# Two-layer macaron kernel, Mamba stage: token normalisation and weighting of expert rows on ScalarE, their addition on VectorE in 512-wide instructions

## The chip, the cores and the metric

The kernel runs on one core of a Trainium2 chip. The metric is the device time of one execution in microseconds (us), taken as the median of several runs. The engines are TensorE (PE in the profile, PEld its weight loads), VectorE (DVE), ScalarE (ACT), GpSimd (POOL) and SyncE (SP), which only issues transfers here.

## The reference, cut to what matters

The input is 4 sequences of 1024 tokens with 128 features. Six blocks follow one another, each added to a running x:

```
x = x + 0.5 * moe(layernorm(x))        # 8 experts, 2 of them per token, and a shared one
x = x + mamba(layernorm(x))            # the stage that is changed: forward and reversed scan
x = x + 0.5 * moe(layernorm(x))
x = x + 0.5 * ternary(layernorm(x))
x = x + attention(layernorm(x))
x = x + 0.5 * ternary(layernorm(x))

layernorm(x) = (x - mean) / sqrt(var + 1e-5)
moe: out = shared(x) + sum over the two chosen experts of w[token, expert] * h[token, expert]
mamba, per direction:
  xs, z = split(h @ in_proj.T);  xs = silu(causal_conv(xs) + b)
  dt = softplus(x_proj(xs) ...);  state = exp(dt * A) * state + dt * xs * B;  y = sum_n state_n * C_n
  y = (y + xs * D) * silu(z);  out = y @ out_proj.T
```

## The kernel before

The tokens lie in SBUF as 32 tiles of 128 tokens (tokens on the partitions), and four tiles make a block of 512. The MoE stage writes each token's two expert outputs to HBM (`orows`), sorted by expert. They are added late: the weighted sum of the first MoE is done inside the Mamba stage, while that stage already runs.

`Returned` holds this return. `fetch` issues one gather on GpSimd for 128 rows into a ring of four buffers; a block takes eight gathers. `combine` (L105 to L118) runs on VectorE: it waits for the eight landings, and then does eight `scalar_tensor_tensor` of 128x128 (row times weight plus x), four for the first expert and, after a wait for these, four for the second. The last one and `s_read` free the ring buffer. The same `combine` is also used by the ternary stage for the second MoE.

The Mamba stage (`mamba`, L1090) makes 16 scan blocks b = 0 to 15: four per sequence (two directions, two halves of 512 tokens), each with 16 slots v, one per state index, and in each slot two halves of the 256 inner channels. A slot is, per half: ScalarE makes exp(dt*A) (`decay`, L1446), eight instructions ahead at most; TensorE broadcasts B into PSUM (`rows`, L1276, two slots ahead, in a ring of three); VectorE multiplies u by B (L1551) and scans (L1527); GpSimd multiplies the state by C (L1634); TensorE adds this to Y in PSUM (`add_y`, L1339). Every engine has its program written out in order, so that the order of the slots is the order of each queue.

Between these, the preparation of later blocks is put in slots by hand. `uses_of` says which use of the one PSUM bank O is in which slot: "T" the transposition of the normalised tokens, "x" the convolution, "z", "xp", "dt" the projections, "out" the output. Steps of the chain have a lag in slots on each engine. The softplus of a "dt" use is four instructions on ScalarE and four of 128x512 on GpSimd (L1660, L1656, L1651, and L1645, which makes u).

At the beginning of a block b, TensorE finishes Y of the block before, does a "dt" use (L1309), and then opens the next Y with matmuls of `diag` and, for the reversed direction, of the saved ys (`open_y`, L1329 and L1331). These can start only when Y has been read: in blocks with b % 4 of 1 and 2 ScalarE has copied Y out (L1453, in its slot 1, behind the "dt" reads and two decays), and in blocks with b % 4 of 3 and 0 VectorE has gated it (`gate`, L1507, behind the scans of its slot 1). The matmul for B of slot 4 (L1276) stands behind `open_y` in TensorE's queue.

The parts that the change touches, all before in VectorE's queue:
- `returned(n)`: 0 and 1 ahead of the scans, 2 to 7 in slots (0,4), (1,6), (2,6), (3,10), (4,10) and (5,10), given as (block, slot) in `RETURNS`.
- `statistics`: mean and variance of the tiles; then GpSimd's `root` (L1604 and L1606) makes 1/sqrt(var+eps), five times in all: twice ahead of the scans and in slots (1,10), (3,14) and (5,14).
- `normalize` (L1497): four `tensor_scalar` of 128x128, SBUF to SBUF. It is called eight times: for the first two blocks of tokens ahead of the scans, and then in slot 0 of scan blocks 2, 3, 6, 7, 10 and 11, for the transposition in slot 2.

Of the kernel before, what the change touches and what calls it, by code (L numbers as in the profile page):

```python
# [10 lines left out]
ALU = mybir.AluOpType  # L11
AX = mybir.AxisListType.X

P = 128
# [31 lines left out]
class Phase:  # L46
# [11 lines left out]
    def sem(self, name):  # L58
        s = self.ctx.enter_context(self.nc.semaphore(f"{self.tag}_{name}"))
        self.sems.append(s)  # L60
        return s
# [23 lines left out]
class Returned:  # L85
# [10 lines left out]
    def fetch(self, pool, ring, s_read, b, n):  # L96
        c, t = n // TPB, n % TPB
        if n == 0 and b >= 4:
            pool.wait_ge(s_read, b - 3)
        col = c * TILES + b * TPB + t  # L100
        pool.indirect_dma_start(ring[:, b % 4, n * P:(n + 1) * P], None, self.orows,
                                bass.IndirectOffsetOnAxis(ap=self.didx[:, col:col + 1], axis=0))\
            .then_inc(self.landed[b % 4], 16)

# [985 lines left out]
def mamba(nc, tag, x, ident, w, back):  # L1090
# [72 lines left out]
    with ExitStack() as ctx:  # L1163
# [45 lines left out]
        s_read = sem("read")  # L1209
# [40 lines left out]
        with nc.Block() as block:  # L1250
# [114 lines left out]
            def _(act):  # L1365
# [7 lines left out]
                act.activation(wzh[:], wi[:, 256:512], ACT.Copy).then_inc(s_wh, 1)  # L1373
                act.wait_ge(s_wc, 1)
# [80 lines left out]
                for b in range(-1, NB + 1):  # L1455
# [5 lines left out]
                    for v in range(NS):  # L1461
                        if v - 1 in uses:
                            o_read(b, v - 1, uses[v - 1])
# [12 lines left out]
            def _(dve):  # L1476
                ch = Chain(dve, s_gch)

                def returned(b):
                    back.combine(dve, ring, s_read, x, b, ch)  # L1480
# [10 lines left out]

                def normalize(tb):
                    i, _, c = place(tb)
                    dve.wait_ge(s_rstd, i + 2 if i else c + 1)
                    for t in range(TPB):
                        tile = i * TPS + c * TPB + t
                        last = dve.tensor_scalar(xn[:, t, :], x[:, tile * P:(tile + 1) * P], mv[:, tile, 0:1],  # L1497
                                                 rstd[:, tile:tile + 1], ALU.subtract, ALU.mult)
                    last.then_inc(s_xn, 1)
# [35 lines left out]
                normalize(0)  # L1535
# [4 lines left out]
                for b in range(-1, NB + 1):  # L1540
                    uses = uses_of(b)
                    for v in range(NS):
# [21 lines left out]
                        if b > 0 and slot_of(b, -2, "T")(v):  # L1564
                            normalize(uses[v + 2][2])
# [11 lines left out]
                        if (b, v) == (-1, 3):  # L1577
# [12 lines left out]
                            normalize(1)  # L1590

            @block.gpsimd
            def _(pool):
# [7 lines left out]
                def root(n):  # L1601
# [3 lines left out]
                    pool.wait_ge(s_ve, n + 1)  # L1605
                    pool.tensor_tensor(rstd[:, t], veps[:, t], mhalf[:, t], ALU.pow).then_inc(s_rstd, 1)  # L1606
# [808 lines left out]
```

## Time and profile before

| | |
|---|---|
| median of 3 runs | 3117.87 us (3114.83 to 3124.79) |
| span of the profiled execution, its one recorded time | 3183.4 us |
| busy in the span | PE 2649.1, DVE 2342.8, ACT 1746.4, POOL 1430.6 us |
| head of the Mamba stage, up to the first scan | about 335 to 400 us of the span |
| its 16 scan blocks | about 400 to 1420 us |
| mean granted TensorE clock | 0.913 |

The profile has one execution. Busy time is the time in which an engine has an instruction running; an instruction that waits inside the engine (for a port, say) counts as busy, one that waits for a semaphore counts as idle. For the idle time the profile names the releaser, the instruction whose end let the engine go on. The times of lines under one another in the timeline are from the start of the span; several instructions of one line that follow each other are one row (xN).

### The profile page before, as it was taken

How to read it: one execution, taken by the hardware profiler on the slowest of the kernel's cores; microseconds unless marked ns; L12 is line 12 of the kernel's file. 1: busy time of each engine (PE TensorE's matmuls, PEld its weight loads, DVE VectorE, ACT ScalarE, POOL GpSimd, SP SyncE). 2: the span in 40 equal slices, each digit the busy share in tenths (PEclk: the TensorE clock that was granted, in tenths of full speed). 3: DMA queues.
4: the chain of work that ended last, by engine and by line, in shares of the span. 5: the costliest groups of instructions: out<-in, count | busy, mean ns of one | idle time of the engine just before them, and what ended most of it. 6: DMA issues, size and time to landing. Idle time of an engine off the chain costs nothing. (4 is left out here: it accounts for less than half of the span.)

```text
span 3183.4 us, 38531 instructions
## 1 busy us (share of the span) xinstructions
PE 2649.1 (83%) x11128; PEld 1684.0 (53%) x11128; DVE 2342.8 (74%) x4109; ACT 1746.4 (55%) x3003; POOL 1430.6 (45%) x1514
## 2 busy tenths in 40 slices
PE   6888378889889989867888589949888889885999
PEld 5666233333334334225766467736555556553877
DVE  6688279989999999987688544477878777764444
ACT  3467365546556646523566345536776667763554
POOL 2465578888878878863464440031211111110000
PEclk9899688989899989996899789969999999996999
DMA  2146222222222222211146200000000000001000
GB/s 66 34 131 133 76 62 64 70 64 72 64 70 72 72 67 70 73 57 54 36 134 115 66 26 1 0 12 1 1 1 2 2 1 1 1 1 37 7 7 13
DMA packets 99373, 146.10 MB, mean 46 GB/s; under 512 B 12892, under 2 KB 50524, under 8 KB 98980
## 3 DMA queue, kind: packets, MB, share of 16 engines
q1 hardware_dynamic: 82052, 98.41, 10.5%
q0 software_dynamic: 16608, 44.78, 6.4%
q8 instruction: 91, 1.49, 0.2%
q14 instruction: 110, 0.90, 0.1%
q10 hardware_dynamic: 512, 0.53, 0.1%
HBM read 124.78 MB, written 18.87 MB: 45 GB/s over the span
## 5 line engine op out<-in xcount | busy, mean ns | idle before, releaser
L1634 POOL TENSOR_TENSOR a_hc<-a_H,a_cb 128x512 f32<-128x512 f32 x512 | 622.4, 1226 | 191.0 <-DVE a_H L1527 160.5
L1339 PE MATMUL a_Y<-a_hc,ident 128*128 128x512 f32 x1024 | 533.1, 640 | 36.8 <-POOL a_hc L1634 34.8
L2074 DVE TENSOR_REDUCE a_mx<-a_W 128x1 f32<-128x512 f32 (+3 forms) x768 | 397.2, 550 | 159.0 <-PE a_W L1878 104.7
L1980 ACT ACTIVATE a_pt<-a_W 128x512 f32<-128x512 f32 (+3 forms) x768 | 353.2, 492 | 227.8 <-PE a_W L1891 224.9
L1446 ACT ACTIVATE a_dA<-a_dt,a_aneg 128x512 f32<-128x512 f32 x512 | 339.7, 714 | 207.9 <-DVE a_H L1527 114.8
L1339 PEld LDWEIGHTS a_Y<-a_hc,ident 128*128 128x128 f32 x1024 | 182.7, 196 | 264.7 <-POOL a_hc L1634 134.8
L1891 PE MATMUL a_W<-a_Q,a_K 128*128 128x512 f32 (+3 forms) x768 | 303.2, 400 | 4.4 <-issue 2.3
L2222 POOL TENSOR_TENSOR a_spare<-a_zero 128x1 f32<-128x1 f32 x128 | 27.1, 212 | 582.7 <-ACT a_pt L1980 582.7
L1875 PE MATMUL a_W<-a_K,a_Q 128*128 128x512 f32 (+3 forms) x768 | 274.9, 365 | 10.8 <-DVE a_mx L2074 10.5
L411 ACT ACTIVATE m_raw<-m_U,m_wg 128x512 f32<-128x512 f32 x248 | 173.6, 701 | 127.7 <-PE m_U L306 122.9
L1009 DVE TENSOR_TENSOR t_hl<-t_raw,t_hh 128x512 fp32r<-128x512 f32 x128 | 88.1, 691 | 209.3 <-ACT t_hh L924 184.6
L1551 DVE TENSOR_TENSOR a_bx<-a_u,a_Bp 128x512 f32<-128x512 f32 x256 | 173.7, 678 | 77.6 <-POOL a_u L1645 41.6
L682 POOL DMA_INDIRECT m_xg<-m_xrows,m_gidx x184 | 194.5, 1057 | 70.4 <-issue 54.9
L1891 PEld LDWEIGHTS a_W<-a_Q,a_K 128*128 128x128 f32 x768 | 146.9, 193 | 143.5 <-issue 67.0
L576 DVE TENSOR_TENSOR m_hl<-m_raw,m_hh 128x512 fp32r<-128x512 f32 x248 | 172.3, 695 | 61.0 <-ACT m_hh L415 50.3
L814 PE MATMUL t_U<-t_hh,t_wh 128*128 128x512 f32 x512 | 204.0, 398 | 0.2 <-issue 0.2
L816 PE MATMUL t_U<-t_hl,t_wh 128*128 128x512 f32 x512 | 202.2, 395 | 0.7 <-issue 0.7
L815 PE MATMUL t_U<-t_hh,t_wl 128*128 128x512 f32 x512 | 202.1, 395 | 0.0
L1907 PE MATMUL a_PV<-a_pt,a_V 128*32 128x512 f32 (+3 forms) x1536 | 168.2, 510 | 40.7 <-POOL a_pt L2225 39.7
L1276 PEld LDWEIGHTS a_Bp<-a_bcs,a_sel 64*128 64x128 f32 x256 | 48.4, 190 | 285.2 <-DVE a_H L1527 176.1
L1276 PE MATMUL a_Bp<-a_bcs,a_sel 64*128 64x512 f32 x256 | 130.5, 511 | 79.7 <-DVE a_H L1527 79.4
L923 ACT ACTIVATE t_raw<-t_U,t_scal 128x512 f32<-128x512 f32 x128 | 88.2, 689 | 194.2 <-PE t_U L816 162.5
(311 smaller groups left out, 6432.0 us busy)
## 6 DMA issues: line engine op xcount, KB each, us to landing
a_cb<-a_crow SPq DMA_DIRECT2D x256, 256.0 KB, 3.2
m_orows<-m_yt SPq DMA_DIRECT2D x46, 256.0 KB
t_wst<-ternary_w SPq DMA_DIRECT2D x22, 256.0 KB, 2.9
m_xrows<-m_pool SPq DMA_DIRECT2D x16, 256.0 KB, 2.3
m_xg<-m_xrows,m_gidx POOLq DMA_INDIRECT x184
out<-x SPq DMA_DIRECT2D x8, 256.0 KB, 2.3
m_wg<-moe_ws SPq DMA_DIRECT2D x2, 516.0 KB, 4.4
a_hc<-mamba_conv_rows SPq DMA_DIRECT2D x1, 1024.0 KB
```

The lines of the kernel that those rows point to most:

```text
L682: pool.indirect_dma_start(xg[:, j % NXG, t * P:(t + 1) * P], None, xrows, bass.IndirectOffsetOnAxis(ap=gidx[:, n:n + 1], axis=0))\
L814: pe.matmul(out, wh[:, piece, c], rhs_h, start=start, stop=False)
L815: pe.matmul(out, wl[:, piece, c], rhs_h, start=False, stop=False)
L816: return pe.matmul(out, wh[:, piece, c], rhs_l, start=False, stop=stop)
L1276: pe.matmul(Bp[:, Q % BRING, :], sel[:, Q % NS, :], bcs[:, Q // NS % 4, :], start=True, stop=True)\
L1339: pe.matmul(Y[:, h, :], ident[:], hc[:, g % HCRING, :], start=False, stop=v == NS - 1).then_inc(s_y, 1)
L1446: act.activation(dA[:, G % ARING, :], dt[:, b % 2, h, :], ACT.Exp, scale=aneg[:, d, h, v:v + 1]).then_inc(s_dA, 1)
L1634: pool.tensor_tensor(hc[:, G % HCRING, :], H[:, s, span], cb[:, v % RING, :], ALU.mult).then_inc(s_hc, 1)
L1875: mm = pe.matmul(out, Q[:, g * GH + j, tile(t)], K[:, g, c * BLK:c * BLK + cols], start=True, stop=not diag)
L1891: pe.matmul(W[:, 3 + u % 3, 0:BLK - r * P], K[:, g, tile(kt)], Q[:, g * GH + j, c * BLK + r * P:(c + 1) * BLK], start=True, stop=True).the ...
L1980: act.activation(pt[:, u % PR, 0:BLK - r * P], W[:, 3 + u % 3, 0:BLK - r * P], ACT.Exp).then_inc(s_exp, 1)
L2074: dve.tensor_reduce(dst, W[:, s % 3, 0:min(BLK, (t + 1) * P - c * BLK)], AX, ALU.max)\
```

## The change

VectorE's `combine` is replaced in the Mamba stage by `weigh` on ScalarE and `add` on VectorE. `weigh` multiplies the fetched rows by the token's weight in the ring buffer itself, with four activations of 128x128 for each of the two experts; `add` adds the weighted rows to x with two `tensor_tensor` of 128x512, the second of which waits for the first. For return n in slot v of VectorE, ScalarE weighs the first expert's rows in slot v-2 and the second's in slot v-1. The ternary stage keeps `combine`.

`normalize` moves to ScalarE, as four `Identity` activations with a scale (rstd) and a bias. The bias is -mean*rstd, which GpSimd's `root` now also makes, with two further instructions, in the place of the variance. Its slots stay; in ScalarE's queue it stands at the beginning of the slot, ahead of that slot's reads of O and its decays. The first one stands ahead of the copy of the convolution weights (L1375), and the second in slot 6 of the block -1, ahead of the read of the "xp" use.

```diff
+    def weigh(self, act, ring, b, c, s_weighed):
+        if c == 0:
+            act.wait_ge(self.landed[b % 4], 32 * TPB * (self.run * NBLK // 4 + b // 4 + 1))
+        for t in range(TPB):
+            n = b * TPB + t
+            at = (c * TPB + t) * P
+            last = act.activation(ring[:, b % 4, at:at + P], ring[:, b % 4, at:at + P], ACT.Copy,
+                                  scale=self.wab[:, c, n:n + 1])
+        last.then_inc(s_weighed, 1)
+
+    def add(self, dve, ring, s_weighed, s_read, x, b, ch):
+        xb = x[:, b * BLK:(b + 1) * BLK]
+        for c in range(2):
+            dve.wait_ge(s_weighed, 2 * b + c + 1)
+            last = dve.tensor_tensor(xb, xb, ring[:, b % 4, c * BLK:(c + 1) * BLK], ALU.add)
+            if c == 0:
+                ch.step(last)
+                ch.join()
+        last.then_inc(s_read, 1)
+        dve.wait_ge(s_read, b + 1)
...
+                def normalize(tb):
+                    i, _, c = place(tb)
+                    act.wait_ge(s_rstd, i + 2 if i else c + 1)
+                    for t in range(TPB):
+                        tile = i * TPS + c * TPB + t
+                        last = act.activation(xn[:, t, :], x[:, tile * P:(tile + 1) * P], ACT.Identity,
+                                              bias=mv[:, tile, 1:2], scale=rstd[:, tile:tile + 1])
+                    last.then_inc(s_xn, 1)
+
+                back.weigh(act, ring, 0, 0, s_weighed)
+                back.weigh(act, ring, 0, 1, s_weighed)
+                normalize(0)
...
+                        for c in range(2):
+                            if (b, v + 2 - c) in RETURNS:
+                                back.weigh(act, ring, RETURNS[b, v + 2 - c][0], c, s_weighed)
+                        if b > 0 and slot_of(b, -2, "T")(v):
+                            normalize(uses[v + 2][2])
+                        if (b, v) == (-1, 3):
+                            back.weigh(act, ring, 1, 0, s_weighed)
+                            back.weigh(act, ring, 1, 1, s_weighed)
+                        if (b, v) == (-1, 6):
+                            normalize(1)
...
                 def returned(b):
-                    back.combine(dve, ring, s_read, x, b, ch)
+                    back.add(dve, ring, s_weighed, s_read, x, b, ch)
...
-                        last = dve.tensor_scalar(xn[:, t, :], x[:, tile * P:(tile + 1) * P], mv[:, tile, 0:1],
-                                                 rstd[:, tile:tile + 1], ALU.subtract, ALU.mult)
...
                     pool.tensor_scalar(veps[:, t], mv[:, t, 1], EPS, None, ALU.add).then_inc(s_ve, 1)
-                    pool.wait_ge(s_ve, n + 1)
-                    pool.tensor_tensor(rstd[:, t], veps[:, t], mhalf[:, t], ALU.pow).then_inc(s_rstd, 1)
+                    pool.wait_ge(s_ve, 3 * n + 1)
+                    pool.tensor_tensor(rstd[:, t], veps[:, t], mhalf[:, t], ALU.pow).then_inc(s_ve, 1)
+                    pool.wait_ge(s_ve, 3 * n + 2)
+                    pool.tensor_tensor(mv[:, t, 1], mv[:, t, 0], rstd[:, t], ALU.mult).then_inc(s_ve, 1)
+                    pool.wait_ge(s_ve, 3 * n + 3)
+                    pool.tensor_scalar(mv[:, t, 1], mv[:, t, 1], -1.0, None, ALU.mult).then_inc(s_rstd, 1)
```

## Rows read from the trace of the kernel before

**Rows 1.** Busy time by stage: window, length, PE, PEld, DVE, ACT, POOL, clock, DMA.
```profile
335.00:400.00 65.00, 19.58 (x43) 9.92 (x43) 17.85 (x59) 21.66 (x35) 46.81 (x47) 0.55 0.29 81
400.00:1420.00 1020.00, 882.61 (x2034) 368.77 (x2035) 959.77 (x1171) 555.77 (x854) 824.08 (x688) 0.92 0.23 68
```

**Rows 2.** What VectorE waited for, 330 to 1425 us: total us, times, longest.
```profile
DVE a_bx L1551 <- POOL a_u L1645: 41.6, 7, 24.0
DVE a_bx L1551 <- PE a_Bp L1276: 35.9, 22, 5.4
```

**Rows 3.** Groups by line and shape, 400 to 1420 us: count, busy us, mean ns.
```profile
L112 DVE SCALAR_TENSOR_TENSOR x<-a_ring,m_wab,x 128x128 f32<-128x128 f32 x48 | 24.8, 577 | 0.2
L1497 DVE TENSOR_SCALAR a_xn<-x,a_mv,a_rstd 128x128 f32<-128x128 f32 x24 | 19.0, 852 | 0.0
```

**Rows 4.** Timeline of three returns (start us, length us), and GpSimd beside the second.
```profile
349.24 2.31 DVE L112 SCALAR_TENSOR_TENSOR x<-a_ring,m_wab,x 128x128 f32<-128x128 f32 x8 [19.74 <-DMA a_ring<-m_orows,m_didx]
...
499.64 5.42 DVE L112 SCALAR_TENSOR_TENSOR x<-a_ring,m_wab,x 128x128 f32<-128x128 f32 x8
501.65 1.29 POOL L1634 TENSOR_TENSOR a_hc<-a_H,a_cb 128x512 f32<-128x512 f32 x1
509.26 1.27 POOL L1634 TENSOR_TENSOR a_hc<-a_H,a_cb 128x512 f32<-128x512 f32 x1 [6.33 <-DVE a_H L1527]
...
732.04 3.13 DVE L112 SCALAR_TENSOR_TENSOR x<-a_ring,m_wab,x 128x128 f32<-128x128 f32 x8
```

**Rows 5.** Timeline of the beginning of block 10, which normalises.
```profile
1061.30 2.51 DVE L1497 TENSOR_SCALAR a_xn<-x,a_mv,a_rstd 128x128 f32<-128x128 f32 x4
...
1067.94 1.61 PE L1329 MATMUL a_Y<-a_xs,a_diag 128*128 128x512 f32 x2 [1.86 <-ACT a_ys L1453]
...
1075.52 0.69 DVE L1551 TENSOR_TENSOR a_bx<-a_u,a_Bp 128x512 f32<-128x512 f32 x1 [1.45 <-PE a_Bp L1276]
```

**Rows 6.** The same of block 14, which does not normalise.
```profile
1304.23 0.67 DVE L1551 TENSOR_TENSOR a_bx<-a_u,a_Bp 128x512 f32<-128x512 f32 x1
...
1310.91 2.08 PE L1329 MATMUL a_Y<-a_xs,a_diag 128*128 128x512 f32 x2 [3.12 <-ACT a_ys L1453]
...
1318.41 0.69 DVE L1551 TENSOR_TENSOR a_bx<-a_u,a_Bp 128x512 f32<-128x512 f32 x1 [3.84 <-PE a_Bp L1276]
```

**Rows 7.** Blocks 11 (which normalises) and 15 (which does not).
```profile
1120.64 2.05 DVE L1497 TENSOR_SCALAR a_xn<-x,a_mv,a_rstd 128x128 f32<-128x128 f32 x4
1127.47 2.08 PE L1329 MATMUL a_Y<-a_xs,a_diag 128*128 128x512 f32 x2 [2.46 <-DVE a_ys L1507]
...
1362.91 0.68 DVE L1551 TENSOR_TENSOR a_bx<-a_u,a_Bp 128x512 f32<-128x512 f32 x1
1367.77 2.08 PE L1329 MATMUL a_Y<-a_xs,a_diag 128*128 128x512 f32 x2 [2.45 <-DVE a_ys L1507]
```

**Rows 8.** Blocks 2 and 3: the two longest normalisations, and block 2's opening of Y.
```profile
545.66 4.57 DVE L1497 TENSOR_SCALAR a_xn<-x,a_mv,a_rstd 128x128 f32<-128x128 f32 x4
554.35 2.08 PE L1329 MATMUL a_Y<-a_xs,a_diag 128*128 128x512 f32 x2 [1.85 <-ACT a_ys L1453]
614.52 3.88 DVE L1497 TENSOR_SCALAR a_xn<-x,a_mv,a_rstd 128x128 f32<-128x128 f32 x4
```

**Rows 9.** Groups by shape that stand nearest to the new instructions: busy us, mean ns.
```profile
L1980 ACT ACTIVATE a_pt<-a_W 128x128 f32<-128x128 f32 x128 | 33.4, 281 | 48.2 <-PE a_W L1891 47.6
L576 DVE TENSOR_TENSOR m_hl<-m_raw,m_hh 128x512 fp32r<-128x512 f32 x248 | 172.3, 695 | 61.0 <-ACT m_hh L415 50.3 <-issue 8.3
L1604 POOL TENSOR_SCALAR a_veps<-a_mv 128x8 f32<-128x8 f32 x3 | 0.8, 250 | 0.0
```

**Rows 10.** Timeline of the head: weight copy, first convolution, read of "xp".
```profile
355.56 1.91 ACT L1375 ACTIVATE a_wch<-a_hc 128x2048 fp32r<-128x2048 f32 x1 [14.07 <-DVE a_hc L1533]
360.88 0.76 PE L1294 MATMUL a_O<-a_xh,a_wch 128*128 128x512 f32 x1 [3.09 <-DVE a_xl L1570]
376.86 0.59 ACT L1394 ACTIVATE a_dbl<-a_O 72x512 f32<-72x512 f32 x1 [2.54 <-PE a_O L1305]
```

More of the change, by code:

```diff
@@ L1208, in mamba @@
         s_gch = sem("gch")
-        s_read = sem("read")
+        s_read, s_weighed = sem("read"), sem("weighed")
         s_pad, s_xn, s_xh = sem("pad"), sem("xn"), sem("xh")
@@ L1490, in statistics @@
                     last.then_inc(s_mv, 1)
[L1492 to L1496, printed above, removed]
-                        last = dve.tensor_scalar(xn[:, t, :], x[:, tile * P:(tile + 1) * P], mv[:, tile, 0:1],
-                                                 rstd[:, tile:tile + 1], ALU.subtract, ALU.mult)
-                    last.then_inc(s_xn, 1)
                 def gate(b):
@@ L1534, in _ @@
                 last.then_inc(s_wc, 1)
-                normalize(0)
                 dve.wait_ge(s_wh, 2)
@@ L1563, in _ @@
                             gate(b - 1)
-                        if b > 0 and slot_of(b, -2, "T")(v):
-                            normalize(uses[v + 2][2])
                         if slot_of(b, 2, "T")(v):
@@ L1589, in _ @@
                             dve.tensor_copy(sel[:], sels).then_inc(s_pre, 1)
-                            normalize(1)
             @block.gpsimd
```

## The prediction

> **What bounds the kernel now.** I read the busy time by stage first. In the head of the Mamba stage (335 to 400 us) no engine is full: a chain of dependent steps sets its length. In the 16 scan blocks (400 to 1420 us) VectorE is busy for 959.77 of 1020 us, GpSimd for 824.08 and ScalarE for 555.77 [rows 1]. VectorE is the bound there, and ScalarE has room. All that the change does lies in these 1085 us; the rest of the span stays as it is.
>
> Second come VectorE's waits. They show where it is not the bound: 41.6 us for GpSimd's u, of which 24.0 are the end of the head and the rest mostly ends of the early blocks, and 35.9 us in 22 waits for TensorE's broadcast of B [rows 2]. Looking for where these 22 stand, I found one around slot 4 of nearly every block. That decides most of what follows: VectorE time that is saved between the start of a block and slot 4 may only lengthen this wait.
>
> Third, the groups by line: 48 weighting instructions take 24.8 us and 24 normalising ones 19.0 us in the scan blocks [rows 3]. That is 577 and 852 ns each, more than they take alone: the eight of return 0, with no compute of GpSimd beside them, take 2.31 us [rows 4]. The timeline of return 3 shows why. It takes 5.42 us, and GpSimd is at work until 501.65+1.29 = 502.94; by the unmerged rows the first of the eight lasts until 503.09. So it sat in the engine until GpSimd had run its queue dry, about 3.1 us [rows 4]. Six returns are 13.9 us of work at 2.31 each, and 10.9 us of such waiting; the normalisations, at about 1.1 us of work each, are 6.6 us of work and 12.4 us of waiting.
>
> **The returns in the scan blocks (six).** Eight instructions become two of 128x512 with two SBUF inputs; such a one takes 0.695 us [rows 9]. With the wait of the second for the first, that is 1.45 us in place of 2.31: 0.86 saved. The wait for GpSimd remains, since the adds, like what they replace, read x and the ring in SBUF. In the three returns where GpSimd has a queue (499.64 and two more of 5 us) I take 0.9 saved. In the other three, as at 732.04 (3.13 us), it is now the first, short instruction that slips in ahead of GpSimd, and the second that waits; the same with the adds gives 0.69 + 1.1 + 0.69 = 2.5, so 0.6 saved. Sum: 3 x 0.9 + 3 x 0.6 = 4.5 us. Bounds: 24.8 - 6 x 1.45 = 16.1 us saved if the adds do not wait at all; 4.8 us lost if the second add of the three long returns has to wait 3.1 us again. All six stand behind slot 4's wait. GpSimd sits idle after them, 6.33 us after return 3 [rows 4], so that it follows VectorE at once, and I count the saving in full.
>
> The Trainium skill's page "SBUF — State Buffer", section "Who interferes with whom", says that `tensor_tensor` with both inputs in SBUF contends with GpSimd's reads, although it has no 2-port mode. By it the saving is that of the remaining waits, 4.5; without it, the 16.1. The trace has no such instruction against a queued GpSimd, only `scalar_tensor_tensor`, which waits. The same section says that the later one blocks until the first one finishes; here it was not one instruction but the whole queue, three of them [rows 4], and the measurement decides.
>
> **Normalisation in blocks 2, 6 and 10.** Here the trace has its own experiment. Blocks 10 and 14 have the same position in their sequence (b % 4 = 2), and block 14 has no normalisation. Counted from what follows the first scan (1061.30 and 1304.23), TensorE opens Y after 6.64 us in block 10 and after 6.68 in block 14, and VectorE gets its B of slot 4 after 14.22 and 14.18 us [rows 5, 6]. Block 10 spent 2.51 us normalising and waited 1.45; block 14 waited 3.84. The removed time comes back as waiting, to within 0.1 us: the chain is GpSimd's last products, TensorE's last adds, "dt", ScalarE's two reads, two decays and the copy of Y. In block 2 Y is opened 554.35 - 545.66 = 8.69 us after that point [rows 8], which is 2 us more than in block 10, because GpSimd is 2 us behind at its start and not because VectorE is. So of 4.57, 3.96 (block 6) and 2.51 us I count 0 as gained. Upper bound: all 11.0.
>
> **Normalisation in blocks 3, 7 and 11.** Here Y is freed by VectorE's own gate, behind the scans of slot 1. Block 11 opens Y 1127.47 - 1120.64 = 6.83 us after its first scan, block 15, without normalisation, 1367.77 - 1362.91 = 4.86 [rows 7]: 1.97 earlier, for 2.05 us of normalising. These are real gains: 2.0 in block 11, 2.0 in block 7 (2.04 there), and of block 3's 3.88 us [rows 8] about 3.8, since Y of block 2 is complete (617.5) before the gate would now come (about 618.1). Sum 7.8 us; lower bound 3.9, if GpSimd's backlog, which the stall lets it work off, takes half.
>
> **What ScalarE takes on.** A 128x128 activation takes 0.281 us [rows 9]. Eight per return and four per normalisation are 6 x 8 + 6 x 4 = 72, some 20 us over the scan blocks, on an engine that idles for 464 us there [rows 1]. What is queued behind them are the decays, which run mostly 6 to 18 us ahead of their scans, and the reads of O. Return 3's two packets stand in slots 4 and 5 of block 1, the others alike. Slot 0's normalisation comes before ScalarE's wait for "dt", in which it idles. The gathers landed long before. Cost 0; if that cover is gone, one packet of 1.1 us in each of six returns, 6.6 us.
>
> **GpSimd's `root`.** Two more instructions of about 0.25 us [rows 9], each behind a semaphore wait of 0.1: 0.65 us. In slots (1,10), (3,14) and (5,14) GpSimd is 2 to 7 us behind, and the end of blocks 1 and 3 and the opening of Y in block 6 wait for it: 3 x 0.65 = 1.9 us lost. Bounds 0 and 4 (if they meet VectorE's port use as well).
>
> **The head.** Weighing and adding return 0 takes, from landing, 4 x 0.28, and then the second four and an add: 2.9 us for 2.31, +0.6. `root` adds 0.65, so rstd comes at 355.7 instead of 354.4, and ScalarE normalises until 356.8. Only then can it copy the weights: 356.8 instead of 355.56 [rows 10]. The subtraction, xl and the first convolution at 360.88 follow: +1.3 us. Return 1 lands 1.2 us later by the same sum (about 368.7), and its eight activations end at 371.0, when the convolution that ScalarE reads next is also ready (371.1). The second normalisation, at about 376.4 to 377.5, ends before the read of "xp" (376.86 + 1.3 = 378.2). So +1.3, with bounds 0.3 and 5.
>
> **Sum.** -4.5 (returns) - 0 - 7.8 (normalisation) + 0 (ScalarE) + 1.9 (`root`) + 1.3 (head) = -9.1 us. In the profiled execution that is 3183.4 to 3174.3. The timed runs have their median at 3117.87, 2.1% under that span; I take the same microseconds there: 3109.
>
> **The rivals.** (1) More is gained: 0.20. Either blocks 2, 6 and 10 gain their 11.0 us too, or the adds don't wait for GpSimd's port (another 11.6); both come to about -20.5, 3097. For it: VectorE is 94% busy, and 44 us of its work are touched. Against it: rows 5 and 6, and what `scalar_tensor_tensor` did.
> (2) GpSimd takes over: 0.23. The stalls were the time in which it caught up, and its lag at the end of blocks 0 to 3 reaches 5 to 7 us. If the returns' and block 3's savings come back as waits for u (-8.3 not had), then -9.1 + 8.3 = -0.8, 3117. Against it: the 6.33 us of idle after return 3.
> (3) Slower: 0.07. The place is the join between the two adds. GpSimd's queue takes the port there, so that the second add of the three long returns waits 3.1 us again (+9.3), and with GpSimd the bound none of the 4.5 + 7.8 is realised: +1.9 + 1.3 + 9.3 = +12.5, 3130. It decides from the point where GpSimd has more queued at the join than it has idle time left in the block. Against it: between scans GpSimd gets new work only from VectorE, which stands still.
> The forecast itself has 0.50.
>
> **Numbers.** About 0.3% (9.4 us) is what this kernel's measurement can tell from no change. The forecast's own range is -4 to -14 and lies across that bound: half of its 0.50 is faster, half the same. Faster 0.25 + 0.20 = 0.45; same 0.25 + 0.23 = 0.48; slower 0.07. The range 3097 to 3121 holds (1) down to its point and (2), and leaves out (3).
>
> **What would show it.** The head: first scan 1 to 2 us later. Returns: two adds in 2.5 to 4.6 us. Blocks 10 and 14 of equal length but for VectorE's xl, with a wait of about 3.9 in both at slot 4; block 2's wait about 7. Blocks 7 and 11 shorter by 2, block 3 by 3 to 4. VectorE's busy time in the scan blocks down by some 23 us, while its wait for B rises by 11. The forecast is wrong if blocks 2, 6 and 10 get shorter by their stalls, if the adds take 1.45 us beside a busy GpSimd, or if the ends of blocks 0 to 3 wait longer for u by what was saved before.

## The result, and the profile after

The changed kernel takes 3106.22 us in the median of 6 runs (3100.84 to 3112.14), the kernel before 3118.59 in 6 runs on the same chip (3114.83 to 3126.70). The ratio is 0.9952, with a 95% interval of 0.9936 to 0.9967: 15 us faster, between 10 and 20 (the medians are 12.4 us apart). The forecast was 3109 (range 3097 to 3121).

The profiled execution of the changed kernel has a span of 3104.3 us, the one of the kernel before 3183.4. Most of these 79 us are not the change: experiment 8 shows a chip on which the kernel before takes this long, with the same stages longer, while its Mamba stage is as long as in the first profile to 1.3 us. The stage is therefore compared directly. From the first load of its weights to the first scan (the head) it takes 66.4 us for 64.8 before, and the 16 scan blocks take 1004.7 for 1019.2. Head and blocks together are 12.9 us shorter.

Busy time by stage (columns as in [rows 1], which it answers):

```profile
312.40:378.70 66.30, 17.90 (x43) 9.24 (x43) 14.33 (x39) 29.76 (x59) 47.43 (x51) 0.58 0.28 80
378.70:1383.50 1004.80, 877.43 (x2033) 366.07 (x2033) 934.85 (x1111) 576.84 (x926) 825.93 (x693) 0.93 0.24 69
```

VectorE has 24.9 us less to do in the scan blocks, ScalarE 21.1 more, and the blocks are 14.4 us shorter. VectorE's waits, 310 to 1390 us, as [rows 2]:

```profile
DVE a_bx L1585 <- PE a_Bp L1297: 43.2, 24, 6.2
DVE a_bx L1585 <- POOL a_u L1680: 41.3, 7, 24.6
DVE x L119 <- ACT a_ring L111: 30.6, 5, 20.9
```

The wait for B has grown from 35.9 to 43.2 us, the one for GpSimd's u has not grown in sum. The third line is nearly all the head. The groups of the moved work in the scan blocks, as [rows 3] and [rows 9]:

```profile
L119 DVE TENSOR_TENSOR x<-x,a_ring 128x512 f32<-128x512 f32 x12 | 19.0, 1586 | 0.6 <-ACT a_ring L111 0.4
L111 ACT ACTIVATE a_ring<-a_ring,m_wab 128x128 f32<-128x128 f32 x48 | 15.2, 389 | 0.0
L1401 ACT ACTIVATE a_xn<-x,a_mv,a_rstd 128x128 f32<-128x128 f32 x24 | 9.8, 478 | 0.0
L1641 POOL TENSOR_SCALAR a_mv<-a_mv 128x8 f32<-128x8 f32 x3 | 0.8, 261 | 0.3
L1639 POOL TENSOR_TENSOR a_mv<-a_mv,a_rstd 128x8 f32<-128x8 f32 x3 | 0.6, 205 | 0.2
```

An add takes 1.59 us in the mean for its 0.70 of work: it still waits for GpSimd. The timeline of return 3 (start, length), as [rows 4], shows it:

```profile
477.50 4.58 DVE L119 TENSOR_TENSOR x<-x,a_ring 128x512 f32<-128x512 f32 x2
479.52 1.28 POOL L1669 TENSOR_TENSOR a_hc<-a_H,a_cb 128x512 f32<-128x512 f32 x1
486.28 1.27 POOL L1669 TENSOR_TENSOR a_hc<-a_H,a_cb 128x512 f32<-128x512 f32 x1 [5.48 <-DVE a_H L1562]
```

GpSimd's queue ends at 480.80, and the first add at 481.36 by the unmerged rows, 0.56 us later, having started at 477.50; the second takes 0.70. The six returns now take 2.17, 4.58, 4.22, 4.17, 2.16 and 2.35 us, where they took 3.12, 5.42, 5.06, 4.97, 3.13 and 3.3: 5.3 us less.

Blocks 10 and 14, what opens Y and what ends the wait at slot 4, as [rows 5, 6]:

```profile
1035.99 2.07 PE L1350 MATMUL a_Y<-a_xs,a_diag 128*128 128x512 f32 x2 [3.12 <-ACT a_ys L1487]
1043.50 0.70 DVE L1585 TENSOR_TENSOR a_bx<-a_u,a_Bp 128x512 f32<-128x512 f32 x1 [3.83 <-PE a_Bp L1297]
...
1274.53 1.81 PE L1350 MATMUL a_Y<-a_xs,a_diag 128*128 128x512 f32 x2 [3.12 <-ACT a_ys L1487]
1282.11 0.70 DVE L1585 TENSOR_TENSOR a_bx<-a_u,a_Bp 128x512 f32<-128x512 f32 x1 [3.89 <-PE a_Bp L1297]
```

Block 10 now waits 3.83 us where it waited 1.45 and normalised for 2.51. Its length is 59.24 us for 59.28 before. Blocks 2 and 3, as [rows 8]; the last line is the end of block 3:

```profile
532.11 2.07 PE L1350 MATMUL a_Y<-a_xs,a_diag 128*128 128x512 f32 x2 [3.12 <-ACT a_ys L1487]
540.68 0.70 DVE L1585 TENSOR_TENSOR a_bx<-a_u,a_Bp 128x512 f32<-128x512 f32 x1 [6.19 <-PE a_Bp L1297]
...
596.28 1.12 PE L1350 MATMUL a_Y<-a_xs,a_diag 128*128 128x512 f32 x2
...
659.45 0.70 DVE L1585 TENSOR_TENSOR a_bx<-a_u,a_Bp 128x512 f32<-128x512 f32 x1 [6.04 <-POOL a_u L1680]
```

Block 11, as [rows 7]. Its first scan starts at 1087.45, and Y is opened 6.03 us later (8.02 before). Counted as in [rows 7], from what follows that scan (1088.63), it is 4.85 us for 6.83; block 15, which never normalised, had 4.86:

```profile
1092.17 1.26 DVE L1542 TENSOR_TENSOR a_ys<-a_zs,a_Y 128x512 f32<-128x512 f32 x2
1093.48 1.66 PE L1350 MATMUL a_Y<-a_xs,a_diag 128*128 128x512 f32 x2 [2.21 <-DVE a_ys L1542]
1101.06 0.70 DVE L1585 TENSOR_TENSOR a_bx<-a_u,a_Bp 128x512 f32<-128x512 f32 x1 [0.53 <-PE a_Bp L1297]
```

The head, as [rows 10]:

```profile
325.86 2.45 ACT L111 ACTIVATE a_ring<-a_ring,m_wab 128x128 f32<-128x128 f32 x8 [7.35 <-DMA a_ring<-m_orows,m_didx]
332.88 1.65 ACT L1401 ACTIVATE a_xn<-x,a_mv,a_rstd 128x128 f32<-128x128 f32 x4 [4.57 <-POOL a_mv L1641]
334.43 1.89 ACT L1409 ACTIVATE a_wch<-a_hc 128x2048 fp32r<-128x2048 f32 x1
339.73 0.76 PE L1315 MATMUL a_O<-a_xh,a_wch 128*128 128x512 f32 x1 [3.98 <-DVE a_xl L1602]
```

In block 0 there is a wait in slot 11 that the kernel before does not have:

```profile
423.20 0.69 DVE L1585 TENSOR_TENSOR a_bx<-a_u,a_Bp 128x512 f32<-128x512 f32 x1 [1.05 <-PE a_Bp L1297]
```

The length of each scan block, before, after and the difference in us:

```
block   0     1     2     3     4     5     6     7     8     9    10    11    12    13    14    15
before 74.76 69.34 68.80 76.82 65.04 62.71 62.19 63.42 57.99 58.65 59.28 64.93 60.08 58.65 58.62 57.88
after  74.51 69.04 67.97 71.58 60.68 62.48 62.73 61.73 60.11 58.65 59.24 61.73 58.91 58.65 58.69 58.03
diff   -0.25 -0.31 -0.83 -5.24 -4.36 -0.23 +0.54 -1.69 +2.12  0.00 -0.04 -3.20 -1.16  0.00 +0.07 +0.15
```

### The profile page after: what moved, and what is told of

The parts are those of the page before. It is cut to its first block and busy times, and to the rows that moved or that the text cites. A ratio compares the mean times of both kernels' runs of the same rounds, so it can differ in the third digit from the quotient of the medians.

```text
span 3104.3 us, 38566 instructions
## 1 busy us (share of the span) xinstructions
PE 2625.7 (85%) x11128; PEld 1673.7 (54%) x11128; DVE 2317.0 (75%) x4029; ACT 1777.0 (57%) x3099; POOL 1427.4 (46%) x1524
## 5 line engine op out<-in xcount | busy, mean ns | idle before, releaser
L1585 DVE TENSOR_TENSOR a_bx<-a_u,a_Bp 128x512 f32<-128x512 f32 x256 | 173.6, 678 | 84.6 <-PE a_Bp L1297 43.2
```

## The experiments

Each starts from the changed kernel. "Blocks" is the length of the 16 scan blocks in the trace of its run: before 1019.2, after 1004.7.

**1. Normalisation alone.** The returns go back to VectorE as one weighting instruction per row tile.

```diff
-                    back.add(dve, ring, s_weighed, s_read, x, b, ch)
+                    back.combine(dve, ring, s_read, x, b, ch)
```

(and ScalarE's five calls of `weigh` are gone.)

> Normalisation on ScalarE and the two further GpSimd instructions, but the returns as in the kernel before (eight weighted adds on VectorE). Theory (saved VectorE time counts only where VectorE stands in the chain): blocks 3, 7 and 11 shorter by 4, 2 and 2 us than before, blocks 2, 6 and 10 as before, +0.9 in the head, +1.9 for GpSimd: -5 us against before, about 0.9984 of it. Rival (VectorE is the bound and all its time counts): -19.0 + 2.8 = -16 us, 0.995.

Measured: 0.9989 (0.9976 to 1.0003) of before; blocks 1011.4, 7.8 shorter. Block 3 is 4.41 shorter, block 7 1.66, block 11 3.19; blocks 2, 6 and 10 change by -0.44, +0.60 and -0.03. The three blocks named gain 9.3 us together; blocks 4, 5, 8 and 12, where at most `root` is changed, differ by -2.2, +2.3, +2.1 and -1.2 (taken up below). The rival's 0.995 lies outside the interval. The time alone cannot be told from that of the kernel before.

**2. Returns alone.** The call moves from ScalarE's loop to VectorE's, and the old `normalize` and `root` are back.

```diff
-                        if b > 0 and slot_of(b, -2, "T")(v):
+                        if b > 0 and not (True) and slot_of(b, -2, "T")(v):
...
+                        if b > 0 and (True) and slot_of(b, -2, "T")(v):
+                            normalize(uses[v + 2][2])
```

> Returns weighed by ScalarE and added in two instructions, normalisation and GpSimd's root as in the kernel before. Theory: 4.5 us less in blocks 0 to 5, +0.6 in the head: -4 us against before, 0.9987. Rival (GpSimd takes the saved time back as waits for u at the ends of blocks 0, 1 and 3): 0 to -1 us. Rival (the adds have no port to wait for): -16 us, excluded already by the trace of after if its adds last 4 us there.

Measured: 0.9992 (0.9979 to 1.0005); blocks 1015.5, 3.7 shorter. The groups in its scan blocks:

```profile
L119 DVE TENSOR_TENSOR x<-x,a_ring 128x512 f32<-128x512 f32 x12 | 19.0, 1585 | 0.6 <-ACT a_ring L111 0.4
L1538 DVE TENSOR_SCALAR a_xn<-x,a_mv,a_rstd 128x128 f32<-128x128 f32 x24 | 19.1, 853 | 0.0
```

The adds cost the same 19.0 us with VectorE's normalisations beside them as without. The blocks with returns, 0 to 5, change by +0.04, -0.84, -2.09, -1.04, -3.14 and -0.96, and blocks 6, 7 and 8, which have none, are longer by 1.57, 1.56 and 2.14. Two of the six savings come back. In block 0 VectorE waits 1.04 us for B in slot 11, a wait that neither the kernel before nor experiment 1 has. After block 5, which is 0.96 shorter, block 6 opens Y 11.67 us after its first scan for 10.70: counted from block 5's first scan it is the same moment, 73.41 us for 73.40. The interval of the timed runs holds no change as well as the forecast of 0.9987.

**3. Only blocks 2, 6 and 10 normalise on VectorE again.**

```diff
-                        if b > 0 and slot_of(b, -2, "T")(v):
+                        if b > 0 and not (b % 4 == 2) and slot_of(b, -2, "T")(v):
...
+                        if b > 0 and (b % 4 == 2) and slot_of(b, -2, "T")(v):
+                            normalize(uses[v + 2][2])
```

> The changed kernel, but the normalisations of blocks 2, 6 and 10 done by VectorE again. Theory: the same time as the changed kernel; VectorE's wait at slot 4 of these blocks goes back from 6.8, 7.9 and 3.8 us to about 2.5, 2.9 and 1.4, and the blocks keep their lengths within 0.5 us. Rival (VectorE is the bound): these blocks are 3.6 us longer each and the whole 11 us longer than the changed kernel.

Measured: 0.9969 (0.9956 to 0.9982); blocks 1006.9. Against the changed kernel, blocks 2, 6 and 10 are -0.49, +0.22 and +0.06 us: the normalising of three blocks, put back, cost nothing. Their waits at slot 4 are 1.96, 3.66 and 1.45 us for 6.84, 7.23 and 3.83. The 2.2 us of the sum are block 4 (+2.47), which has no edit. Block 10, after its first scan:

```profile
1036.60 2.54 DVE L1541 TENSOR_SCALAR a_xn<-x,a_mv,a_rstd 128x128 f32<-128x128 f32 x4
...
1050.86 0.69 DVE L1594 TENSOR_TENSOR a_bx<-a_u,a_Bp 128x512 f32<-128x512 f32 x1 [1.45 <-PE a_Bp L1297]
```

The wait is 1.45 us again, to the hundredth that of [rows 5].

**4. Only blocks 3, 7 and 11 normalise on VectorE again.** The same edit with `b % 4 == 3`.

> The changed kernel, but the normalisations of blocks 3, 7 and 11 done by VectorE again. Theory: blocks 3, 7 and 11 are longer than in the changed kernel by 4, 2 and 2 us, as their gate comes later by that: +8 us in all. Rival (no normalisation in slot 0 is worth anything, the gain of blocks 3 and 11 came from TensorE's clock): the same time as the changed kernel.

Measured: 0.9986 (0.9975 to 0.9997); blocks 1013.9, 9.2 longer than the changed kernel's. Block 3 +5.39, block 7 +3.29, block 11 +3.04: 11.7 us. Block 8 is 3.65 shorter, so that blocks 7 and 8 together gain nothing from the normalisation's move: 121.5 us here, 121.8 in the changed kernel, 121.4 before. Block 11:

```profile
1100.10 2.05 DVE L1541 TENSOR_SCALAR a_xn<-x,a_mv,a_rstd 128x128 f32<-128x128 f32 x4
1106.93 2.07 PE L1350 MATMUL a_Y<-a_xs,a_diag 128*128 128x512 f32 x2 [2.46 <-DVE a_ys L1551]
1115.56 0.70 DVE L1594 TENSOR_TENSOR a_bx<-a_u,a_Bp 128x512 f32<-128x512 f32 x1 [1.58 <-PE a_Bp L1297]
```

With the 2.05 us of normalising, 1.05 us more of waiting at slot 4 come back (1.58 for 0.53). That is the part which the forecast did not have.

**5. The adds read PSUM.** In returns 2 to 7 the second operand is a PSUM tile; this kernel leaves out the adding of those returns' expert rows, and its time is to be read so.

```diff
-            last = dve.tensor_tensor(xb, xb, ring[:, b % 4, c * BLK:(c + 1) * BLK], ALU.add)
+            other = bx[:, 1, :] if bx is not None else ring[:, b % 4, c * BLK:(c + 1) * BLK]
+            last = dve.tensor_tensor(xb, xb, other, ALU.add)
...
-                    back.add(dve, ring, s_weighed, s_read, x, b, ch)
+                    back.add(dve, ring, s_weighed, s_read, x, b, ch, bx if b > 1 else None)
```

> The changed kernel, but the adds of returns 2 to 7 read their second operand from PSUM (a product tile) instead of the ring, so that each has one SBUF input; the expert rows of these six returns are fetched and weighed but not added, which this kernel leaves out. Theory (the adds' time above 1.45 us per return is the wait for GpSimd's port, as both operands are in SBUF): the six returns take 1.3 to 1.5 us each instead of 19.0 in all, GpSimd keeps its backlog and idles less behind them; the saved 10 us count, since GpSimd still runs dry in the block: 8 to 10 us under the changed kernel. Rival (GpSimd takes the time back at the ends of blocks 1 to 3): the adds get as short, but the waits for u grow and the total falls by 3 us or less. Rival (no port: the adds are long for another reason): they stay at 4.2 to 4.6 us in returns 3 to 5.

Measured: 0.9913 (0.9889 to 0.9938); blocks 992.8, 11.9 shorter than the changed kernel's. Return 3 and the group:

```profile
502.51 1.38 DVE L120 TENSOR_TENSOR x<-x,a_bx 128x512 f32<-128x512 f32 x2
503.32 1.27 POOL L1687 TENSOR_TENSOR a_dt<-a_rl,a_um 128x512 f32<-128x512 f32 x1
508.09 1.27 POOL L1670 TENSOR_TENSOR a_hc<-a_H,a_cb 128x512 f32<-128x512 f32 x1 [2.26 <-DVE a_H L1563]
...
L120 DVE TENSOR_TENSOR x<-x,a_bx 128x512 f32<-128x512 f32 x12 | 8.1, 674 | 0.6 <-ACT a_ring L111 0.5
```

Beside a GpSimd at work the two adds take 1.38 us, not 4.58. Of VectorE's time 10.9 us are gone, and all of it shows in the length (10.5 us against the changed kernel's second trace, experiment 9). So the adds' wait is the one for the port between GpSimd and two SBUF inputs, as the Trainium skill's page "SBUF — State Buffer", section "Who interferes with whom", says of `tensor_tensor`. GpSimd did not take over either: the adds of blocks 1, 2 and 3 take 3.2, 2.8 and 2.8 us less, and the blocks are shorter by 4.4, 3.6 and 2.8 against the first trace of the changed kernel and by 3.2, 2.7 and 2.8 against experiment 9's. GpSimd's idle time after return 3 fell from 5.48 to 2.26.

**6. GpSimd's `root` away from the slots where it is late.**

```diff
-        ROOTS = {(1, 10): 2, (3, 14): 3, (5, 14): 4}
+        ROOTS = {(1, 10): 2, (4, 3): 3, (6, 3): 4}
```

> The changed kernel with GpSimd's roots of slots (3,14) and (5,14) in slots (4,3) and (6,3), where nothing waits for them at once. Theory (they lie in GpSimd's backlog ahead of the block's end): block 3 shorter by 2.6 us, its wait for u down from 6.0 to about 3.5; block 6's opening of Y, at +11.2 us, earlier by up to 2.6; 3 to 5 us in all. Rival (GpSimd's root is hidden): no block changes by more than 0.5 us.

Measured, in one run with its trace (3165.65 us, for 3188.77 of the kernel before on the same chip): blocks 999.3, 5.4 shorter. Block 3 is 68.86 us for 71.58, block 6 60.49 for 62.73, the two blocks whose end or opening waited for it; but block 4, behind block 3, is 2.25 us longer, so that blocks 3 and 4 together gain only 0.5. The end of block 3, for the 6.04 us above:

```profile
679.34 0.69 DVE L1585 TENSOR_TENSOR a_bx<-a_u,a_Bp 128x512 f32<-128x512 f32 x1 [3.31 <-POOL a_u L1680]
```

**7. GpSimd issues the gathers in slots 1 to 8 of every block.** They stood in the odd slots up to 15.

```diff
-                        if v >= 7 if b < 0 else v % 2:
+                        if v >= 7 if b < 0 else 1 <= v <= 8:
```

> The changed kernel with GpSimd's gathers in slots 1 to 8 of each block instead of every second slot up to 15: four of them, 1.2 us each, leave the second half, where GpSimd falls behind. Theory (the waits for u and B at the ends of blocks 0, 1 and 3, 11.5, 3.5 and 6.0 us, are GpSimd's backlog): they shrink by up to 4.9 us each, 8 to 14 us in all, little of it lost in the first half, where GpSimd has slack. Rival (GpSimd's sum of work in the block decides, wherever it stands): the waits move to the middle of the blocks and the scans last as long, within 2 us.

Measured, in one run with its trace (3184.00 us, for 3188.77; outside the Mamba stage, the first ternary and the attention stage are 324.4 and 828.3 us, for 316.7 and 820.7 in experiment 6): blocks 996.9, 7.8 shorter, just under the 8 to 14 expected, and 6.4 shorter than experiment 9's. The end waits fell from 11.46 to 7.89 in block 0 (both with a wait in slot 11), from 3.50 to 1.08 in block 1 and from 1.25 to 0 in block 2. Block 3, against the expectation, is 1.3 us longer. Its end and a scan within it:

```profile
645.38 1.28 DVE L1562 TENSOR_TENSOR_SCAN a_H<-a_dA,a_H,a_bx 128x512 f32<-128x512 f32 x1 [1.13 <-POOL a_hc L1669]
...
680.39 0.70 DVE L1585 TENSOR_TENSOR a_bx<-a_u,a_Bp 128x512 f32<-128x512 f32 x1 [4.75 <-POOL a_u L1680]
```

With eight issues close together in the first half, one scan waits for GpSimd's product (1.13 us), VectorE waits 0.53 at slot 4 where it did not, and the adds of return 5 take 4.78 us for 4.17; the end wait fell only by 1.29. What is saved at the end is paid there and more.

**8. The kernel before, again, on the chip of experiments 5 to 7.** No edit.

> The kernel before, unchanged, profiled once more. Its first profile has a span of 3183 us against runs of 3118 us, and its two MoE stages and first ternary stage are 20 us longer each than in every profile of the other kernels. Theory (that one execution was slow outside the Mamba stage, for a reason that no kernel has to do with): now about 3117 us, with stages of 312, 305 and 297 us outside and the Mamba stage within 5 us of 1094. Rival (the kernel before is really longer there, and the change shortens these stages): they are 335, 326 and 316 us again.

Measured: span 3184.3, time 3186.08. The theory was wrong, and of the rival only the numbers held. The long span was not one slow execution, since it came again; nor does it belong to the kernel before, since experiments 5 to 7 show the same stages as long on this chip. Stage lengths in us (first mixture, head, blocks, tail, second mixture, first ternary, attention, second ternary):

```
before       335.6   64.8  1019.2   10.3   325.6   316.4   824.6   286.8
again (8)    335.9   64.4  1018.4   10.2   328.6   325.1   816.6   285.1
after        312.4   66.4  1004.7   10.3   304.8   298.5   821.9   285.3
exp. 5       337.3   66.8   992.8     .    326.2   319.7      .       .
exp. 9       315.8   66.9  1003.3     .    304.4   298.4   826.3      .
```

The kernel before ran at 3188.77 on this chip (median of 7) and at 3118.59 where the changed one was timed. Between the traces of the two places, the two mixtures and the first ternary stage differ by 6 to 9% (337.3 and 312.4, 326.2 and 304.8, 325.1 and 298.5), where the change does nothing. The Mamba stage is 1093.0 us here and 1094.3 in the first profile, and experiments 5 to 7, on this chip, fit in with it. What makes the other stages longer was not tried. Within the Mamba stage this second trace of the same kernel differs from the first in two blocks: block 7 takes 65.10 us for 63.42 and block 8 56.46 for 57.99.

**9. The changed kernel again.** No edit.

> The changed kernel once more, on the same chip as the two that follow, as their base. Expected ratio to the kernel before 0.995 to 0.997 (-14 us in the scans, +1.5 in the head, of 3118).

Measured: 3111.70 against 3123.30, 0.9960 (0.9945 to 0.9975); blocks 1003.3, 1.4 us from the first trace. Blocks 0, 1 and 2 are 75.40, 67.86 and 67.00 us, for 74.51, 69.04 and 67.97: about 1 us of a single block there is not the kernel's.

**10. Both moves of GpSimd's work**, with block 3's gathers left in the odd slots.

```diff
-        ROOTS = {(1, 10): 2, (3, 14): 3, (5, 14): 4}
+        ROOTS = {(1, 10): 2, (4, 3): 3, (6, 3): 4}
...
-                        if v >= 7 if b < 0 else v % 2:
+                        if v >= 7 if b < 0 else v % 2 if b == 3 else 1 <= v <= 8:
```

> The changed kernel with both moves on GpSimd: the roots of (3,14) and (5,14) in (4,3) and (6,3), and the gathers in slots 1 to 8, except in block 3, where they stay in every second slot (early ones made block 3 longer by 1.3 us). Theory (GpSimd's backlog at the ends of the early blocks is what the blocks wait for, and the two moves act in different blocks): blocks 0 to 2 shorter by 2.3, 3 and 2 us, block 3 by 2.7, block 6 by 2.2: 11 to 13 us under the changed kernel, 0.9955 to 0.9965 of it, 0.991 to 0.993 of the kernel before. Rival (the moves take from the same slack): no more than the larger of the two alone, 5 to 8 us.

Measured: 3100.20 us, 0.9921 (0.9907 to 0.9935); blocks 994.1. That beats both kernels: 25 us under the kernel before by the ratio, some 12 under the changed one run beside it. Blocks 0, 1, 2, 3 and 6 are 71.53, 65.40, 65.71, 69.49 and 60.41; block 4 has 3.2 us more than in experiment 9. In the traces the gain over experiment 9 is 9.2 us, in the timed runs 12, for 11 to 13 expected and 5 to 8 by the rival. What block 3 gains (2.1) is lost again in block 4.

**11. The same, with the head's normalisation after the weight copy on ScalarE.**

```diff
-                normalize(0)
                 act.wait_ge(s_wc, 1)
                 act.activation(wcv[0], taps, ACT.Copy).then_inc(s_wh, 1)
+                normalize(0)
```

> As the one before, and ScalarE copies the convolution weights before it normalises the first tokens. Theory (the changed kernel's head is 1.5 us longer because that copy waits for the normalisation): the copy starts as soon as VectorE's products are done, about 1 us earlier; the transposed tokens come 1.6 us later, but they had 1.5 us to spare against the weights' subtraction; the head is 0.5 to 1 us shorter. Rival (the transposed tokens are then the late ones): the head is 0 to 1 us longer.

Measured: 3096.81 us, 0.9922 (0.9907 to 0.9937), the ratio of experiment 10; head 67.1 us for 67.3, blocks 996.1 for 994.1 (blocks 0 and 1, not edited, 1.0 and 1.3 longer), from landing to the first convolution 13.45 us for 13.87 in the changed kernel. Nearly all of the expected gain is missing. The timeline of ScalarE, TensorE and VectorE there:

```profile
335.53 1.91 ACT L1408 ACTIVATE a_wch<-a_hc 128x2048 fp32r<-128x2048 f32 x1 [4.81 <-DVE a_hc L1568]
...
337.35 1.63 ACT L1401 ACTIVATE a_xn<-x,a_mv,a_rstd 128x128 f32<-128x128 f32 x4
...
340.25 0.60 ACT L1420 ACTIVATE a_xh<-a_O 128x512 fp32r<-128x512 f32 x1 [1.12 <-PE a_O L1309]
340.88 0.69 DVE L1602 TENSOR_TENSOR a_xl<-a_O,a_xh 128x512 fp32r<-128x512 f32 x1 [0.78 <-ACT a_xh L1420]
341.72 0.76 PE L1315 MATMUL a_O<-a_xh,a_wch 128*128 128x512 f32 x1 [1.50 <-DVE a_xl L1602]
```

The weights are ready sooner, but the tokens, normalised behind the copy, now come last: transposed, read as "xh" and as "xl", they let the convolution start where the weights did before.

**Traces and times together.** The Mamba stage of each trace (its difference to before, as a share of 3119 us) against the ratio that the timed runs gave:

```
                       head + blocks   by the trace   timed (95%)
1 normalisation alone      -7.2           0.9977      0.9989 (0.9976 to 1.0003)
2 returns alone            -2.9           0.9991      0.9992 (0.9979 to 1.0005)
3 blocks 2, 6, 10 back     -9.9           0.9968      0.9969 (0.9956 to 0.9982)
4 blocks 3, 7, 11 back     -2.8           0.9991      0.9986 (0.9975 to 0.9997)
changed kernel            -12.9           0.9959      0.9952 (0.9936 to 0.9967)
9 the same again          -13.8           0.9956      0.9960 (0.9945 to 0.9975)
10 roots and gathers      -22.6           0.9928      0.9921 (0.9907 to 0.9935)
11 the same, head         -20.8           0.9933      0.9922 (0.9907 to 0.9937)
5 adds read PSUM          -24.4           0.9922      0.9913 (0.9889 to 0.9938)
```

All agree within the intervals, so the trace's account of this one stage is enough for the time. The two halves alone make -10.1 of the whole's -12.9, but not block by block: against their sum the whole is longer by 1.7 us in block 2 and by 1.0 in blocks 4 and 12, and shorter by 1.6, 1.6, 1.6 and 2.1 in blocks 5 to 8. Block 8 is 2.1 us longer than before in each half and in the whole. What these differences hang on is taken up at the end of the next section.

## Why the prediction was right, and where a size was off

The time came out inside the range, 15 us for 9.1, and the two mechanisms of the forecast (the adds still wait for GpSimd; VectorE's time counts only where nothing else waits behind it) are what the runs show. That the sum came so near is partly luck: two returns gave nothing and were counted in full, and faster openings of Y, which the sum did not have, outweigh this.

**Returns: VectorE's time right, two of six wrongly counted in full.** Predicted 4.5 us of VectorE's time, measured 5.3. The first add waits until GpSimd's queue is dry, and experiment 5 takes exactly this wait away. The three short returns (3.12 to 2.17, 3.13 to 2.16, 3.3 to 2.35) saved 0.95 each and not 0.6: their wait is now 0.7 us over the adds' 1.45, where 1.1 was taken (0.9 for the third). The long ones saved 0.8 each, for 0.9. The forecast's step that all six stand behind slot 4's wait, so that the saving counts in full, failed for two. Return 2 stands in slot 4 of block 0, and its 0.95 us are the new wait of 1.05 in slot 11: TensorE works there without a gap on two convolutions (409.6 to 422.7 us), and B of slot 11 stands behind them in its queue. Return 7 stands in block 5, and block 6 opens Y no sooner for it, as experiment 2 shows: TensorE's last adds to Y wait there for GpSimd, which has no idle time from 782.9 to 792.3 us in experiment 2. That is the forecast's rival (2) in one place. Returns 3 to 6 gave 3.4 us.

**Normalisation in blocks 2, 6 and 10: right.** Predicted 0 for 11.0 us removed; measured -0.83 (which is return 4's 0.84 in that block), +0.54 and -0.04, with the waits at slot 4 up from 2.45 to 6.84, from 2.92 to 7.23 and from 1.45 to 3.83 (the first two as the sum of the waits in slots 2 and 4). Experiment 3 puts the work back and gets waits of 1.96, 3.66 and 1.45. Blocks 10 and 14 of the kernel before had said this to 0.1 us.

**Normalisation in blocks 3, 7 and 11: the mechanism right, the term too small.** Predicted 3.8 + 2.0 + 2.0 = 7.8; measured 5.2 + 1.7 + 3.2 = 10.1, and 11.7 by experiment 4. (In block 3 return 5's saving of 0.80 and `root`'s cost of 0.76 are in the 5.2 too and cancel.) Block 7's 1.7 is not certain: the kernel before takes 63.42 us there in one trace and 65.10 in the other, and block 8 takes the 1.7 back. Y is opened at +6.04, +6.03 and +6.03 us from the first scan for +9.86, +8.03 and +8.02: this is the forecast's term to 0.1. The rest goes with the length of the matmuls, that is with TensorE's clock. Opening Y is a row of fp32 matmuls of 128x512, 1.06 us each at 1.2 GHz and 0.59 at 2.4. In block 11 the eight took 1.22, five times 1.06, 0.87 and 0.59 before; they take 0.81, three times 1.06, 0.95 and three times 0.59 after. In block 3 five of the eight were slow and none is now. TensorE stood 2.44 us before them in block 3 and 2.46 in block 11; now it does not stand in block 3 and stands 2.21 in block 11. The granted clock of these openings, before and then after (block 3, then block 11; the third column from the right):

```profile
623.20:629.30 6.10, 6.10 (x9) 2.69 (x10) 6.10 (x8) 3.19 (x5) 4.09 (x4) 0.60 0.34 78
1127.40:1133.60 6.20, 6.13 (x8) 2.66 (x9) 6.20 (x9) 3.19 (x5) 3.51 (x4) 0.52 0.21 68
```

```profile
596.20:600.00 3.80, 3.80 (x10) 1.80 (x10) 3.80 (x6) 3.80 (x7) 3.29 (x4) 1.00 0.41 86
1093.40:1098.80 5.40, 5.32 (x9) 2.30 (x10) 5.40 (x8) 3.77 (x6) 2.76 (x3) 0.68 0.21 68
```

The forecast counted the opening's shift and not the speed of what is opened. Block 11's slot 4 waits for these matmuls, so it gained 1.99 + about 1.2. That experiment 4 brings block 11's 3.04 us back with the stand of 2.46 and the opening's 2.07 us shows the connection; that the shorter stand, and nothing else in the order of TensorE's work, makes the clock higher was not tried alone.

**ScalarE: 0, right,** although its instructions cost more than the 0.281 us taken: 0.389 each for weighing and 0.478 for normalising. The 0.281 came from an exponential without a scale or bias per partition; these have one and two such operands. The 25.0 us in the scan blocks stayed beside other work: VectorE's adds wait for them 0.4 us in all.

**`root`: 1.9 predicted, about 1.8 measured.** The ends of blocks 1 and 3 wait 0.7 and 0.76 us longer (3.50 for 2.80; 6.04 for 5.28), and in experiment 2, with the old `root`, they wait 2.80 and 5.31. In block 6 Y opens 0.53 us later from the first scan; counted from block 5's first scan, against experiment 2, it is 0.3. Experiment 6 shows that the whole `root`, its 1.7 us of `pow` included, was on the path there, which is more than the change added.

**The head: +1.3 predicted, +1.6 measured** (+2.0 to +2.5 in the traces of experiments 3 to 7 and 9 to 11), and the term itself was too small. From landing to the first convolution it is 339.73 - 325.86 = 13.87 us, for 360.88 - 349.24 = 11.64 before: +2.2. Of this, weighing and adding is 0.9 (3.24 us for 2.31; 0.6 predicted), `root` 0.9 (2.32 us for 1.46; 0.65 predicted) and the normalisation before the copy 1.55 us, of which 0.5 shows (1.1 was taken, at 0.28 an instruction instead of 0.39 from start to start). What follows the first convolution is 39.0 us, for 39.6 before; in the second trace of each kernel it is 39.5 and 39.2, so the lower total of the first trace is within what two traces of one kernel differ by.

**The rivals.** (1) More is gained: the sum came 4 us beyond the forecast by the traces and 6 by the time, but by neither of its two ways: experiment 3 excludes the one, the 19.0 us of the adds the other. (2) GpSimd takes over: apart from return 7, no. The end waits of blocks 1 and 3 rose by 1.5 us, which is `root`, and experiment 5 took another 10.5 to 11.9 us out with GpSimd beside it. (3) fell with it: in the three long returns the second add takes 0.69 us (in the others it is the one that waits, 1.05 to 1.65). Of the signs named, VectorE's wait for B was to rise by 11 us and rose by 7.3: blocks 2, 6 and 10 wait 11 longer, and blocks 3, 4, 11 and 12 wait less.

**What is left over.** Blocks 3, 7 and 11 are 10.1 us shorter. The returns of blocks 1, 2, 4 and 5 save 3.6, block 0 is 0.3 shorter, and 1.8 come back in blocks 1, 5 and 6, through `root` and GpSimd's lag; small differences in blocks 10, 14 and 15 add 0.2. That is 12.0 of the blocks' 14.4 us. The rest is in openings that no edit touches: block 4 (-3.4 beside its return; its waits at slots 4 and 6 fell from 5.18 to 1.77), block 12 (-1.2) and block 8 (+2.1). The granted clock from block 4's first scan to its opening of Y is 0.51 before and 0.83 after:

```profile
690.10:703.40 13.30, 12.34 (x20) 6.24 (x21) 12.71 (x16) 2.80 (x5) 10.57 (x10) 0.51 0.21 66
```

```profile
661.80:671.60 9.80, 8.51 (x20) 4.81 (x21) 9.80 (x14) 2.76 (x5) 7.86 (x8) 0.83 0.21 60
```

Block 8 shows that such a difference needs no change of the kernel: it takes 57.99 us before and 60.11 after, but 56.46 in experiment 4 and, with the kernel before itself, 56.46 in experiment 8. The clock from its first scan to its opening is 0.82 before (943.5 to 952.9 us). In experiment 4, in the changed kernel and in experiment 8 it is 1.00, 0.55 and 1.00:

```profile
924.50:932.30 7.80, 5.87 (x18) 3.33 (x19) 7.80 (x11) 2.75 (x5) 4.87 (x5) 1.00 0.25 68
```

```profile
909.40:920.90 11.50, 10.75 (x20) 5.05 (x19) 11.50 (x16) 2.79 (x5) 7.49 (x7) 0.55 0.25 69
```

```profile
944.70:952.50 7.80, 5.90 (x18) 3.33 (x19) 7.80 (x11) 2.73 (x5) 4.85 (x5) 1.00 0.20 67
```

So 2 to 4 us of a block go with whether TensorE's matmuls there run at 1.2 or 2.4 GHz, and two executions of one kernel can differ in it. What decides it was not settled. About 2.4 us of the measured gain are therefore not explained by the change's own steps, and not excluded from it either: block 4 is short in both traces of the changed kernel and long in both of the kernel before.

## What to carry to other kernels

Before counting a removed instruction as gained, look for the next wait behind it on the same engine, and for a sibling iteration that never had the instruction: blocks 14 and 15 here said 0 for 2.5 us of work and 2.0 for 2.05, and for the moment at which Y is opened both held. Look for that wait beyond the block too: the first and the last return were lost to one seven slots later and one in the next block. Where the wait is for matmuls, read at which clock they ran, because moving their start can change their length too. And where a second engine is near its limit, when it issues its side work (8 gathers, a `pow`) was worth 9 to 12 us here, nearly as much as the change itself.

## What the runs showed of the hardware

- An add of two SBUF operands on VectorE (128x512 fp32), 0.69 us by itself, took 3.85 when GpSimd had work queued, and ended 0.56 us after the last of it; with one operand in PSUM two of them took 1.38 beside the same work (return 3, experiment 5). The Trainium skill's page "SBUF — State Buffer", section "Who interferes with whom", has the later one wait for the first to finish; here it waited for all that was queued.
- A 128x128 fp32 activation from SBUF to SBUF with a scale per partition took 0.389 us, with scale and bias 0.478, against 0.281 for the one from PSUM in [rows 9], which has neither. The second such operand is 0.089 us; what the first costs and what the memory does is not separated here.
- One chip ran the kernel before at 3188.77 us, where the other experiments' two had 3119.82 and 3123.30 and the first comparison 3118.59. The difference lies in the two mixture stages and the first ternary stage, whose traces are 6 to 9% apart; the timed ratios on the faster chips agree with Mamba stages compared across them.
- One kernel, run twice, had a granted clock of 0.82 and of 1.00 from block 8's first scan to its opening of Y, and the block took 57.99 and 56.46 us (first profile and experiment 8).
